# The order of a transformer tower's first loads: embedding weights split, GpSimd's loads held back, nine ones fewer

## The reference, cut to what matters

```python
patches = _patchify(x, PATCH)                          # (16, 36, 768), 768 = channel, row, column
tok = jnp.einsum('bnd,de->bne', patches, W_emb) + b_emb
tok = jnp.concatenate([cls, tok], axis=1) + pos_embedding
h = jnp.concatenate([cls_tok, tok], axis=1)            # 38 tokens an image
h = h + attention(layernorm(h))                        # blends three kinds of bands, uses anchor_q
h = h + experts(layernorm(h))
```

## Time and profile before

| | |
|---|---|
| median of 3 runs | 223.77 us (223.25 to 223.87) |
| the profiled execution | 222.36 us |
| its span, first to last instruction | 220.6 us |
| TensorE busy | 207.4 us, 94% of the span |
| VectorE, ScalarE, GpSimd busy | 55%, 41%, 31% |
| products of ones (L599) | 250 records, 38.0 us |

### The profile page before, as it was taken

How to read it: one execution, slowest core, us unless ns; L and a number is a source line. 1 busy time by engine, 2 the same in 40 slices (tenths; PEclk the granted TensorE clock), 3 DMA queues, 4 the chain that set the end, 5 groups by cost and what they waited for, 6 DMA issues and landing times.

```text
span 220.6 us, 5435 instructions
## 1 busy us (share of the span) xinstructions
PE 207.4 (94%) x1918; PEld 182.6 (83%) x1918; DVE 120.5 (55%) x340; ACT 89.9 (41%) x255; POOL 68.9 (31%) x90
## 2 busy tenths in 40 slices
PE   7999899899999999999968969999999999999993
PEld 7998698677768668778856849999999999999982
DVE  2153247757576656565587956677664333344312
ACT  2163855543234444323267915533343333433220
POOL 5007052083050605025277500022243231532220
PEclk9999999999999999999999696999999999999999
DMA  6999999999992000001044479844324322342124
GB/s 129 198 240 186 175 303 258 295 325 329 282 304 87 5 3 4 3 0 47 3 122 109 123 173 269 276 121 57 48 46 70 56 42 46 54 66 23 20 36 155
DMA packets 25159, 28.06 MB, mean 127 GB/s; under 512 B 2730, under 2 KB 21917, under 8 KB 25133
## 3 DMA queue, kind: packets, MB, share of 16 engines
q1 hardware_dynamic: 21037, 24.11, 41.8%
q0 software_dynamic: 3472, 2.75, 8.8%
q10 hardware_dynamic: 624, 0.85, 1.9%
HBM read 16.90 MB, written 9.23 MB: 118 GB/s over the span
## 4 chain that ended last, share of the span: by engine, by line
PE 57%; DMA 24%; DVE 6%; ACT 6%; issue 6%; DVEq 0%; SPq 0%; POOLq 0%; ACTq 0%
DMA sums<-ys,xs 22%; PE ps L599 13%; PE ps L625 5%; PE ps L1054 5%; PE ps L730 4%; PE ps L1077 4%; PE ps L869 3%; PE ps L769 2%; PE ps L762 2%; PE ps L849 2%; PE ps L744 2%; DMA h<-sums 1%; PE ps L617 1%; PE ps L734 1%; PE ps L935 1%
## 5 line engine op out<-in xcount | busy, mean ns | idle before, releaser
L1824 POOL DMA_INDIRECT sums<-ys,xs x15 | 23.2, 1546 | 62.9 <-DMA sums<-ys,xs 38.1
L599 PE MATMUL ps<-ones 128*128 128x128 f32 x250 | 38.0, 304 | 2.2 <-DVE ones L1142 1.2
L599 PEld LDWEIGHTS ps<-ones 128*128 128x128 f32 x250 | 33.9, 212 | 3.9 <-ACT kT L1639 1.5
L1077 PE MATMUL ps<-w2s,hidT 128*128 x204 | 36.1, 326 | 0.0
L1077 PEld LDWEIGHTS ps<-w2s,hidT 128*128 128x128 f32 x204 | 33.1, 189 | 0.9 <-issue 0.3
L1054 PE MATMUL ps<-w1hi,xhi 128*128 x68 | 25.0, 367 | 2.0 <-DVE xhi L1461 1.9
L1709 ACT ACTIVATE ys<-ps,xs 128x192 f32<-128x192 f32 x17 | 7.1, 420 | 40.6 <-PE ps L1077 40.6
L1460 DVE TENSOR_TENSOR xlo<-ps,xhi 128x128 fp32r<-128x128 f32 x17 | 5.0, 291 | 29.0 <-ACT xend L1702 28.9
L1781 POOL DMA_INDIRECT sent<-row,index x12 | 13.8, 1148 | 13.1 <-DVE index L1336 6.3
L1054 PEld LDWEIGHTS ps<-w1hi,xhi 128*128 128x128 f32 x68 | 13.1, 193 | 3.1 <-issue 3.1
L1795 POOL TENSOR_TENSOR vm<-vtok,cst 114x576 f32<-114x576 f32 (+1 forms) x12 | 14.2, 1182 | 1.0
(11 more groups left out here) (202 smaller groups left out, 403.4 us busy)
## 6 DMA issues: line engine op xcount, KB each, us to landing
sent<-blank SPq DMA_DIRECT2D x1, 5289.0 KB, 33.8
w2s<-in_L_ffn_W SPq DMA_DIRECT2D x8, 576.0 KB, 7.9
w1s<-in_L_ffn_W SPq DMA_DIRECT2D x4, 768.0 KB, 17.1
xs<-sent SPq DMA_DIRECT2D x17, 129.0 KB, 2.1
w1s<-in_L_ffn_W SPq DMA_DIRECT2D x4, 384.0 KB, 18.3
w1hi<-w1hi SPq DMA_DIRECT2D x8, 192.0 KB, 3.6
ximg<-in_x SPq DMA_DIRECT2D x12, 96.0 KB, 6.6
w1s<-in_L_ffn_b SPq DMA_DIRECT2D x1, 792.0 KB
```

What stands on the lines that cost most here:

```text
L599: pe.matmul(bank[:, 0:128], ones[:, 0:128], ones[:, 0:128], start=True, stop=True)
L1077: last = pe.matmul(ps[6 + j % 2][:, 0:D], hidT[:, k, :], of_expert(w2s[:, :, k, :], expert), start=(k == 0), stop=(k == FCH - 1))
L1824: po.indirect_dma_start(sums, bass.IndirectOffsetOnAxis(ap=xs[:, j % NS, WIDE + 1:].bitcast(U32), axis=0), ys[:, j % NY, :], None, compute ...
```

## The change

`wemb` is loaded in two pieces. The first two parts (`SOON` = 2) keep their place between channels 1 and 2; the other four are a load of their own behind channel 2, with a semaphore of its own, `wemb_rest`. TensorE waits for it ahead of part 2's products, and SyncE waits for it, in place of the first piece, ahead of the experts' bias. GpSimd waits for the whole of channel 0 before it issues its five small loads. The products of ones go from 30 to 24 before the first transpose and from 10 to 7 after part 1.

```diff
--- before.py
+++ after.py
@@ -64,7 +64,8 @@
 EMPTY = E * REGION
 PASS = DF // 2
 AHEAD = 4
-WARM = 30
+WARM = 24
+SOON = 2
 HEAD = 128
 TAIL = D - HEAD
 WIDE = D + TAIL
@@ -312,6 +313,7 @@
         consts_in = sem("consts_in")
         x_in = [sem(f"x_in{c}") for c in range(CH)]
         wemb_in = sem("wemb_in")
+        wemb_rest = sem("wemb_rest")
         qkvw_in = sem("qkvw_in")
         outw_in = sem("outw_in")
         pos_in = sem("pos_in")
@@ -502,10 +504,11 @@
         def _(sp):
             for c in range(CH):
                 if c == CH - 1:
-                    sp.dma_start(wemb[:], w_emb.rearrange("(k p) c -> p k c", p=128)).then_inc(wemb_in, 16)
+                    sp.dma_start(wemb[:, 0:SOON], w_emb[0:SOON * 128].rearrange("(k p) c -> p k c", p=128)).then_inc(wemb_in, 16)
                 for i in range(GRID):
                     if i % 3 < 2:
                         load_rows(sp, c, i)
+            sp.dma_start(wemb[:, SOON:], w_emb[SOON * 128:].rearrange("(k p) c -> p k c", p=128)).then_inc(wemb_rest, 16)
             sp.dma_start(cst[:, 128:], consts[:, 128:LOADED]).then_inc(consts_in, 16)
             sp.wait_ge(dv_posb_zero, 1)
             sp.dma_start(posa[0:1, :], cls_tok.rearrange("a b d -> (a b) d")).then_inc(pos_in, 16)
@@ -517,7 +520,7 @@
             sp.dma_start(wgs[:], wg.rearrange("(i p) e -> p i e", p=HALF)).then_inc(wg_in, 16)
             sp.dma_start(b2s[:], b2).then_inc(wg_in, 16)
             sp.wait_ge(x_in[CH - 1], 16 * GRID)
-            sp.wait_ge(wemb_in, 16)
+            sp.wait_ge(wemb_rest, 16)
             sp.dma_start(b1s[:], b1).then_inc(b1_in, 16)
             sp.dma_start(w1s[TAIL:END, :, 1, :], b1.partition_broadcast(END - TAIL)).then_inc(b1_in, 16)
             for e in range(0, E, 2):
@@ -632,6 +635,8 @@
                 if k == 0:
                     pe.wait_ge(wemb_in, 16)
                     pe.wait_ge(dv_class_zero, 1)
+                if k == SOON:
+                    pe.wait_ge(wemb_rest, 16)
                 pe.wait_ge(dv_patches, k + 1)
                 pe.wait_ge(ac_patches, k + 1)
                 for g in range(2):
@@ -640,7 +645,7 @@
             for k in range(KCH):
                 turn_patches(k)
                 if k == 1:
-                    hold_clock(ps[4], 10)
+                    hold_clock(ps[4], 7)
                 if k >= 2:
                     first_parts(k - 2)
                 if k == 3:
@@ -1736,6 +1741,7 @@
         @block.gpsimd
         def _(po):
             linked = {}
+            po.wait_ge(x_in[0], 16 * GRID)
             for k, w in enumerate((w_loc, w_str, w_glo)):
                 po.dma_start(wv[:, k:k + 1], w.partition_broadcast(GTOK)).then_inc(wv_in, 16)
             for i in range(2):
```

## The result

The changed kernel takes **228.31 us** (median; 227.36 to 230.04), the kernel before 223.51 beside it: a ratio of 1.0195, 95% interval 1.0148 to 1.0242, some 4.4 us slower (the two medians lie 4.8 us apart). The prediction said 222.9 and, for the range, 221.9 to 224.3. The direction is that of rival C, the size more than twice C's. The profiled execution took 228.33 us, its span is 225.5 instead of 220.6, and its mean granted clock (the share of TensorE's full speed) 0.968 instead of 0.985.

The account below looks back on a forecast made before the run. TensorE's chain bounds the first 22 us: fewer ones save 2.04 us, channel 1's landing leaves 1.40, the wait for qkvw 0.87. Taken from the runs' median of 223.77, that gives 222.9 us, range 221.9 to 224.3.

Parts of the forecast that it names:

- rival C: Anchor loads fly as long as before, 7.6 us, landing at 17.7; engines stand, 2.0 us slower, 225.8; chance 0.11.
- the anchors' flight: GpSimd's second anchor load, issued at about 10.13, flies 4.5 us and lands at 14.6, 0.3 us late.
- D: TensorE's clock falls to 1.2 GHz for one more stretch after 0.5 us idles; 1.03 us back, 223.9; chance 0.06.
- First and second hold: Fewer ones before TensorE's transposes save 1.36 and 0.68 us, 2.04 together; channel 1's landing at 11.4 leaves 1.40.
- Weights: First two parts land at 12.1, the other four at 15.4, wanted at 16.2; the new wait costs nothing.
- Rival E: Reordering does nothing, channel 2 still lands at 15.4; hidden behind qkvw, same 222.9; chance 0.45 together with the forecast.
- Rival B: VectorE's channel 0 copy holds back GpSimd's issues; anchors at 15.3, gain 0.41, 223.4; chance 0.20, shared with qkvw 0.42 later.
- the end of the forecast: At L664 TensorE waits for qkvw, landing at 20.87, and starts at 20.92; 0.87 us of gain are left.
- A: qkvw lands by 20.4 and isn't the bound; 1.40 us stay, 222.4, or up to 2.04, 221.7; chance 0.18.
- Noise: About 0.3% (0.67 us) is what a measurement tells from no change; faster means below 223.1, chance 0.56.

Follow-up runs that it names:

- e4: Changed kernel without GpSimd's wait for channel 0: 223.49 us, ratio 0.9972 to the kernel before.
- e3: Kernel before with six and three ones fewer as its only edit: 224.04 us, ratio 1.0035.
- e11: Changed kernel without GpSimd's wait for channel 0, once more in another set of runs: ratio 0.9922 to the kernel before.
- e7: Changed kernel with the anchors' features computed after channel 2's copies instead of after channel 1's: 224.06 us, ratio 0.998 to the kernel before.
- e2: Kernel before with the split of the weights as its only edit: 222.17 us, ratio 0.9919.
- e10: Kernel before with the split of the weights as its only edit, once more in another set of runs: ratio 0.9964.
- e6: Changed kernel; SyncE waits for channel 0 before issuing channel 2, and GpSimd issues the anchors first: 223.45 us, ratio 1.0035 to the kernel before.
- e12: Changed kernel with anchors' features after channel 2, and the 37-row position table loaded as 1 and 36 rows: 222.99 us, ratio 0.9941 to the kernel before.

## Why the prediction was wrong

**The step that failed** is the anchors' flight, as put: "How long does it fly? [...] I take 4.5, between 3.8 and 5.3 [...] The ends are 13.9 and 17.7." It flew 8.6 to 8.8 us and landed at 19.67, outside even the far end (17.7, which belongs to a flight of 7.6; the 5.3 of the stated bounds gives 15.4). I priced it as a property of the load and of how many queues were busy, and said that one busy queue less would shorten it. It didn't get shorter: without the wait, in e4, it is 8.2 to 9.1. The packets show, as far as the rows above reach, that it is set by what was issued before it. The rows of before already said so: the anchors, issued at 3.1 to 3.7, flew 6.9 to 7.6 us, and image loads issued at 3.5 to 4.0 flew 6.8 to 7.4. A 4.5 KB load that takes as long as a 96 KB load beside it isn't flying, it stands in line. Issued 7.3 us later (10.38 instead of 3.11), it came behind more than 2.4 MB; in the kernel before 1.31 MB had moved when its second half began.

The rule of the Trainium skill that I set against rival C (DMA: Bandwidth & Descriptors, "Queues, rings and completion order"), turns between queues packet by packet, doesn't describe what is seen here: with at most two other queues at work, and from 11.1 us on SyncE's alone, a third with five small loads got no packet until 16.9. The measurement decides; whether the five already stood in their queue by then, the profile doesn't show.

**C and D were priced apart.** C's working (the stand ends with the anchors, everything follows) was right and its end 2 us short. D asked for a clock fall from two gaps of half a microsecond. The stand of C made a gap of 3.83 us, and the fall came from it, at 2.86 us in the front where D had 1.03.

**First and second hold.** The transposes came at 9.21 (predicted 9.0), the second copy waited for the image's DMA as said, but until 12.99 instead of 11.5, so the third pair came at 13.73 (12.24). The arithmetic of the ones was right and the landing wasn't a constant: channel 1 was taken between 11.76 and 13.19 in the runs where VectorE waited for it. The 2.04 us of ones bought nothing in e3.

**Weights.** No wait on them at the third part, as predicted. The four parts were to land at 15.4; SyncE's wait for them and for channel 2 ended at 18.21 in the kernel after, at 15.56 in e11 and 17.08 in e4. In the kernel after it was the stand that hid this, which is luck: the forecast wanted them at 16.2. Only in e7, without a stand, does the new wait touch the path: there they landed at some 16.9 and the third part's products begin at 16.94, 0.65 us after the start of the fifth pair instead of the usual 0.55. "Costs nothing" held to 0.1 us. Rival E had the order at nothing; that it wins a little is likely by e2 and e10 and not shown.

**Rival B** falls: GpSimd's first issue took 0.73 us at 8.58, begun inside VectorE's copy (8.38 to 9.07), and 0.73 before. The hold that the Trainium skill, SBUF — State Buffer, "Who interferes with whom", would let one expect isn't seen in this row.

**qkvw (the end of the forecast, and A).** In the kernel after it landed at 9.18 + 15.1 = 24.3 instead of 20.87, and nobody waited for it, since the front was later still. In e7 and e6 it was the bound, as the forecast had it, at 23.07 and 22.12 instead of 20.92.

**Noise.** The prediction took 0.3% for what a measurement tells from no change. The intervals reach 0.4 to 1.0 points to either side, so a gain of 0.87 us, 0.4%, could hardly have been told from nothing here.

## What to carry to other kernels

Before a load is issued later, add up the bytes that will then have been issued ahead of it on every queue; a small load whose flight equals that of the large ones beside it is in line, and here an issue 7.3 us later made the second half of the anchors land 8.4 us later (19.67 instead of 11.2). Where an engine will stand for it, price the idle of TensorE behind it together with the clock at which it resumes, not as two rivals. And landings of one profiled execution have a spread: a gain of 1 us that rests on two of them needs a second profile.

## What the runs showed of the hardware

- Five GpSimd loads of 0.4 to 4.5 KB, issued from 8.0 to 10.9 us in four kernels, moved nothing until 2.37 to 2.44 MB issued earlier had moved; with less issued ahead they began at 1.78 MB (e6) and 0.36 MB (before).
- After TensorE had idled 3.83 us the granted clock was 0.51 and 0.64 in the next two stretches of 4 us. With 32 records of ones more in the same gap it was 1.00.
- With GpSimd's wait, VectorE took channel 0 at 7.61 to 8.38 us (seven kernels), without it at 8.34 to 9.36 (six profiles of four kernels) and at 7.79 in the profile of before. Without small loads among them the images may come a microsecond sooner; one profile of each doesn't settle it. It won nothing here, since the later channels set the pace.
- A 37-row table in one load or as 1 + 36 rows ahead of a 432 KB load: 13.9 (e7) or 10.0 us (e12) for the latter to land, with 11.2 to 15.3 in all profiles that have one load and this order. What the division changes on the way wasn't shown.
